# Graph attention on one core: the exponentials go to PSUM alone, and VectorE reads and copies them from there

## The chip, the core and the metric

The kernel runs on one NeuronCore of a Trainium2 chip. The core has TensorE for matrix products, VectorE and ScalarE for elementwise work, GpSimd, here only for issuing gathers, and SyncE, here only for issuing plain transfers. Each engine works through its own queue of instructions in order and waits for others by semaphores. The metric is the device time of one execution in microseconds. Before the change it is 2854.36 us, the median of three runs (2850.2 to 2856.99).

## The reference

A graph of 6250 nodes has 206,250 edges, sorted by the node they end in, with 128 features for each node and each edge, and 8 heads of 16 columns. For each edge a score per head is computed, clipped and exponentiated; the exponentials weigh the source node's values, both are summed by target node and divided, and the result is added to the node's features and normalised.

```python
Qh, Kh, Vh = (h @ WQ), (h @ WK), (h @ WV)          # each reshaped to (N, 8, 16)
Eh = (edge_attr @ WE).reshape(-1, H, D)
score = jnp.einsum('ehd,ehd,ehd->eh', Kh[src], Qh[dst], Eh) * inv_sqrt_d
score = jnp.exp(jnp.clip(score, -5.0, 5.0))
msg = Vh[src] * score[:, :, None]
wV = jax.ops.segment_sum(msg, dst, num_segments=N)
Z = jax.ops.segment_sum(score, dst, num_segments=N)
h_out = wV / (Z[:, :, None] + 1e-06)
...
x = _layernorm(x + h_out.reshape(N, H * D), axis=-1)
```

## The kernel before

A first stage, some 170 us long, projects the nodes and writes tables of K with V and of Q to HBM. The main loop then takes the edges in 403 groups of 512, four tiles of 128 edges each. Its order is written out by hand, engine by engine, and each engine's part is a function `step(g)`.

GpSimd issues four indirect transfers for a group (`gather`, L536), which fetch a row of K and V for each edge into `kv`, a ring of 20 groups. Before the first of them it waits for `msg_ok`, which says that the messages of the group that had that buffer are made. SyncE loads the edge features `attr` (L316) when TensorE has turned older ones, and rows of Q (L322).

In `step(g)` TensorE turns the edge features of group g+2 (L651, to bank `psT`), computes distances to nearby nodes (L659, `psF`), multiplies the turned features of group g+1 by the weights (L667, `psE`), selects rows of Q (L677, `psQ`) and, last, sums the messages of group g-1 by target node (L687, from `hot` and `msg` to the first 136 columns of one of two banks `psW`). That last product waits for `msg_ok`, and it counts `sums` up.

ScalarE copies and marks for group g+2 (L832, L838), takes the exponential of the clipped scores of group g (L844), and prepares `hot`, the 0/1 matrix of targets, for group g+2 (L821 four times, L826).

VectorE multiplies K of group g by the edge product in `psE` (L1056), adds the sums of group g-2 from `psW` to `acc` (L1093 twice), multiplies by the selected Q in `psQ` (L1061), makes the messages of group g-1 (L1077), reduces to scores (L1066) and clips (L1072). Between these stand small instructions of `finish`, which complete one window of 128 nodes in each turn of eight groups. Once in a turn VectorE loads eight window numbers into its registers (L283).

`msg` has two buffers of 4 x 136 columns in SBUF for each partition: 128 columns of messages and 8 of exponentials for each tile. TensorE needs both side by side. Before the change ScalarE writes the exponentials straight into the 8 columns, and VectorE reads them there as the second input of the messages.

Of the kernel before, what the change touches and what calls it, by code (L numbers as in the profile page):

```python
# [5 lines left out]
P = 128  # L6
# [5 lines left out]
ACT = mybir.ActivationFunctionType  # L12
AX = mybir.AxisListType

HEADS = 8
# [11 lines left out]
MSGS = 2  # L27
# [19 lines left out]
def graph_attention_layernorm(nc, x, src, dst, edge_attr, wq, wk, wv, we, out):  # L47
# [12 lines left out]
    n_nodes, dim = x.shape  # L60
    n_edges = src.shape[0]
    TILES = 4
    GROUP = TILES * P
# [6 lines left out]
    DH = dim // HEADS  # L70
    MW = dim + HEADS
    SCALE = float(DH) ** -0.5
# [33 lines left out]
    with ExitStack() as ctx:  # L106
        def sb(name, shape, dt=F32):
            return ctx.enter_context(nc.sbuf_tensor(name, shape, dt))

        def pb(name, shape):  # L110
            return ctx.enter_context(nc.psum_tensor(name, shape, F32))

        def sem(name):
            return ctx.enter_context(nc.semaphore(name))
# [18 lines left out]
        msg = sb("msg", [P, MSGS, TILES, MW])  # L133
        score = sb("score", [P, TILES * HEADS])
        clipped = sb("clipped", [P, TILES * HEADS])
# [51 lines left out]
        psW = pb("psW", [P, 2, GROUP])  # L187
# [65 lines left out]
        exp_ok = sem("exp_ok")  # L253
        msg_ok = sem("msg_ok")
        sums = sem("sums")
# [25 lines left out]
        def load_row(engine, row, g, n, largest):  # L281

            _, values = nc.values_load_multi_w_load_instructions(  # L283
                table[0:1, row, bass.ds(g + COLUMN[row], n)], engines=(engine,), min_val=0, max_val=largest)
            return values

        def per_head(ap):
            return ap.rearrange("p t (h d) -> p t h d", h=HEADS)
# [4 lines left out]
        def _(sp):  # L293
# [36 lines left out]
            def load_bases(g, n):  # L330
                return load_row(mybir.EngineType.SP, BASE, g, n, PARTS * (n_nodes - NEAR))
# [405 lines left out]
        def _(act):  # L737
# [101 lines left out]

            def exponentials(g):  # L840
                act.wait_ge(clip, g + 1)
                if g >= MSGS:
                    act.wait_ge(sums, g - MSGS + 1)
                nc.scalar.activation(msg[:, g % MSGS, :, dim:MW], clipped[:, :].rearrange("p (t h) -> p t h", h=HEADS),  # L844
                                     ACT.Exp, scale=SCALE).then_inc(exp_ok, 1)

            def step(g):
                if g + 2 < G:
                    copy_attr(g + 2)
                    mark_near(g + 2)  # L850
                exponentials(g)
                if g + 2 < G:
                    mark(g + 2)
# [28 lines left out]
        def _(dve):  # L882
# [191 lines left out]

            def messages(g):
                dve.wait_ge(exp_ok, g + 1)
                nc.vector.tensor_tensor(per_head(msg[:, g % MSGS, :, 0:dim]), per_head(kv[:, g % RINGS, :, dim:2 * dim]),  # L1077
                                        msg[:, g % MSGS, :, dim:MW].unsqueeze(3).to_broadcast([P, TILES, HEADS, DH]),
                                        ALU.mult).then_inc(msg_ok, 1)

            def load_windows(g, n):

                half_windows = load_row(mybir.EngineType.DVE, HALF_WINDOW, g, n, 2 * (WIN - 1))
                return [((h + 1) // 2, h // 2) for h in half_windows]
# [58 lines left out]
            def step(g, windows, w=None):  # L1143
                u = g % TURN

                def meanwhile(i):
                    if i == 0 and g >= 2:
                        add_sums(g - 2, windows)
                    if i == 1 and g >= 1:
                        messages(g - 1)  # L1150
                    if w is not None and 3 * u + i < STAGES:
                        finish(3 * u + i, w, 1, window_y[:, :, :], finished, w * STAGES)

                scores(g, meanwhile)
# [17 lines left out]
            for g in range(B_LAST * TURN, G):  # L1172
                step(g, windows[g - B_LAST * TURN])
            messages(G - 1)
            add_sums(G - 2, windows[-2])
            add_sums(G - 1, windows[-1])
# [90 lines left out]
```

## Time and profile before

| What | Value |
|---|---|
| Median of three runs | 2854.36 us |
| The profiled execution's own time | 2860.5 us |
| Its span | 2858.7 us |
| TensorE busy (matrix products) | 1845.5 us, 65% |
| VectorE busy | 1490.2 us, 52% |
| ScalarE busy | 1373.7 us, 48% |
| GpSimd busy | 1581.0 us, 55% |
| Mean granted TensorE clock | 0.743 of full speed |
| Memory traffic | 125 GB/s mean |

A busy time is the sum of an engine's recorded instructions. No engine is busy for more than two thirds of the span, so the time is made of chains between engines, and an average share says little. What is to be read is who waits for whom at each point of a step. A row of a timeline gives the start in us, the duration in us, engine, line, operation, output<-inputs, the count of merged instructions and, in brackets, how long the engine had been idle before and what released it. In a row of a grouped view the two numbers after the bar are total busy us and mean ns of one.

### The profile page before, as it was taken

What the parts mean: (1) busy time and instruction counts of PE and PEld (TensorE: products, weight loads), DVE (VectorE), ACT (ScalarE), POOL (GpSimd) and SP (SyncE); (2) the same over time, 40 slices, a digit from 0 to 9 for tenths busy, and PEclk for the clock granted to TensorE, in tenths of its full rate; (3) what the DMA queues carried; (4) which work ended last, traced back from release to release, by engine and by line L of the source; (5) the groups of instructions that cost most, each with busy time, mean ns of one, the idle gap of its engine ahead of it and who ended that gap; (6) DMA issues with size and microseconds to landing.
All of it is one profiled execution on the core that took longest, in us unless ns stands there. A gap on an engine that the chain in (4) does not pass through costs nothing.

```text
span 2858.7 us, 39244 instructions
## 1 busy us (share of the span) xinstructions
PE 1845.5 (65%) x10440; PEld 1536.1 (54%) x10441; DVE 1490.2 (52%) x3796; ACT 1373.7 (48%) x3309; POOL 1581.0 (55%) x1629
## 2 busy tenths in 40 slices
PE   6266766767667666566666667566656676666676
PEld 5255655555555555455555555455555565555565
DVE  4154455555555555555554555555555555555567
ACT  3144554444544544454444444444444454444455
POOL 7435565555555555555555555555555565555540
PEclk9677677676777777777777777877777777777678
DMA  8335444444444444444444444444444444444431
GB/s 244 104 114 166 126 131 121 124 121 126 126 124 124 125 126 120 122 126 124 121 125 119 120 122 125 127 119 126 124 121 124 118 131 124 122 126 124 122 114 38
DMA packets 281405, 356.25 MB, mean 125 GB/s; under 512 B 144640, under 2 KB 177615, under 8 KB 281186
## 3 DMA queue, kind: packets, MB, share of 16 engines
q0 software_dynamic: 76864, 209.29, 24.9%
q1 hardware_dynamic: 203746, 144.18, 18.1%
q8 instruction: 88, 1.44, 0.2%
q14 instruction: 131, 1.07, 0.1%
q10 hardware_dynamic: 576, 0.26, 0.0%
HBM read 337.59 MB, written 15.97 MB: 124 GB/s over the span
## 4 chain that ended last, share of the span: by engine, by line
PE 61%; issue 33%; another core or an unknown queue 3%; DVE 1%; ACT 1%; DVEq 0%; DMA 0%; SPq 0%; ACTq 0%
PE psW L687 22%; PE psE L667 19%; PE psT L651 9%; PE psF L659 6%; PE psQ L677 4%; PE psE L610 1%; ACT hot L821 0%; PE psW L619 0%; DVE acc L1022 0%; DVE kv L901 0%; DVEq L283 0%; ACT hotT L838 0%; DMA hot<-in_x_dram 0%; ACT q_stage L793 0%
## 5 line engine op out<-in xcount | busy, mean ns | idle before, releaser
L536 POOL DMA_INDIRECT kv<-kv_table,src_idx x1580 | 1539.7, 975 | 1173.2 <-DVE msg L1077 736.8
L687 PE MATMUL psW<-msg,hot 128*128 128x136 f32 x3224 | 677.2, 373 | 891.7 <-issue 889.2
L687 PEld LDWEIGHTS psW<-msg,hot 128*128 128x128 f32 x3224 | 585.9, 264 | 935.4 <-issue 927.8
L1093 DVE TENSOR_TENSOR acc<-psW,acc 64x136 f32 x806 | 239.0, 296 | 860.6 <-remote 668.9
L667 PE MATMUL psE<-w_e,attrT 128*128 128x128 f32 x3224 | 590.6, 339 | 3.0 <-DVE prod L1056 3.0
L832 ACT ACTIVATE attrT<-psT 128x512 f32<-128x512 f32 x403 | 239.8, 595 | 727.8 <-remote 694.1
L667 PEld LDWEIGHTS psE<-w_e,attrT 128*128 128x128 f32 x3224 | 505.5, 239 | 138.8 <-issue 138.8
L821 ACT ACTIVATE hot<-iota,local 128x128 f32<-128x128 f32 x1612 | 509.0, 387 | 0.0
L1056 DVE TENSOR_TENSOR prod<-kv,psE 128x512 f32<-128x512 f32 x403 | 275.7, 684 | 363.1 <-issue 146.1
L844 ACT ACTIVATE msg<-clipped 128x32 f32<-128x32 f32 x403 | 92.3, 229 | 603.7 <-DVE clipped L1072 473.9
L651 PE MATMUL psT<-ident,attr 128*128 128x128 f32 x1612 | 348.1, 357 | 2.1 <-ACT kv L766 0.9
L826 ACT ACTIVATE hot<-hot,one 128x512 f32<-128x512 f32 x403 | 290.9, 722 | 13.1
L651 PEld LDWEIGHTS psT<-ident,attr 128*128 128x128 f32 x1612 | 283.3, 191 | 3.5 <-issue 3.3
L1061 DVE TENSOR_TENSOR prod<-prod,psQ 128x512 f32<-128x512 f32 x403 | 277.2, 688 | 12.6
L838 ACT ACTIVATE hotT<-psF,near_bias 128x512 bf16<-128x512 f32 x403 | 275.4, 683 | 12.3 <-remote 10.5
L1077 DVE TENSOR_TENSOR msg<-kv,msg 128x512 f32<-128x512 f32 x403 | 276.7, 687 | 0.3 <-ACT msg L844 0.3
L1066 DVE TENSOR_REDUCE score<-prod 128x32 f32<-128x512 f32 x403 | 271.4, 673 | 0.0
L659 PE MATMUL psF<-feats,coef 3*128 3x512 bf16 x403 | 201.8, 501 | 2.0 <-ACT hotT L838 1.6
L677 PE MATMUL psQ<-q_near,hotT 128*128 128x128 bf16 x1612 | 175.3, 233 | 18.5 <-issue 17.3
L677 PEld LDWEIGHTS psQ<-q_near,hotT 128*128 128x128 bf16 x1612 | 140.5, 108 | 28.5 <-issue 17.8
L659 PEld LDWEIGHTS psF<-feats,coef 3*128 3x128 bf16 x403 | 38.3, 95 | 107.8 <-issue 104.2
L1072 DVE TENSOR_SCALAR clipped<-score 128x32 f32<-128x32 f32 x403 | 76.7, 190 | 4.6
(111 smaller groups left out, 466.1 us busy)
## 6 DMA issues: line engine op xcount, KB each, us to landing
attr<-in_edge_attr_dram SPq DMA_DIRECT2D x403, 256.0 KB
kv<-kv_table,src_idx POOLq DMA_INDIRECT x1580
q_near<-q_table SPq DMA_DIRECT2D x403, 32.0 KB
kv_table<-kv SPq DMA_DIRECT2D x12, 512.0 KB
q_table<-q_stage SPq DMA_DIRECT2D x12, 384.0 KB
hot<-in_x_dram SPq DMA_DIRECT2D x12, 256.0 KB
xT<-in_x_dram SPq DMA_DIRECT2D x8, 384.0 KB
out_dram<-xT SPq DMA_DIRECT2D x45, 64.0 KB
```

The lines of the kernel that those rows point to most:

```text
L536: nc.gpsimd.indirect_dma_start(out=kv[:, g % RINGS, t, :], out_offset=None, in_=kv_table, in_offset=bass.IndirectOffsetOnAxis(ap=src_idx[: ...
L651: last = nc.tensor.transpose(psT[:, t * P:(t + 1) * P], attr[:, g % ATTRS, t, :], ident[:, :])
L659: nc.tensor.matmul(psF[:, :], coef[:, :], feats[:, g // FEATS % 2, g % FEATS, :], start=True, stop=True)\
L667: last = nc.tensor.matmul(psE[:, g % 2, t * P:(t + 1) * P], attrT[:, g % 2, t * P:(t + 1) * P], w_e[:, :], start=True, stop=True)
L677: last = nc.tensor.matmul(psQ[:, g % 2, t * P:(t + 1) * P], hotT[:, g % 2, t * P:(t + 1) * P], q_near[:, g % QROWS, :], start=True, stop=True)
L687: last = nc.tensor.matmul(psW[:, g % 2, 0:MW], hot[:, g % HOTS, t, :], msg[:, g % MSGS, t, :], start=(t == 0), stop=(t == TILES - 1))
L821: last = nc.scalar.activation(hot[:, g % HOTS, t, :], iota[:, :], ACT.Abs, scale=-1.0, bias=local[:, t, g:g + 1])
L826: nc.scalar.activation(slot, slot, ACT.Relu, scale=-1.0, bias=one[:, 0:1]).then_inc(hot_ok, 1)
L838: nc.scalar.activation(hotT[:, g % 2, :], psF[:, :], ACT.Relu, bias=near_bias[:, 0:1]).then_inc(hotT_ok, 1)
L1056: nc.vector.tensor_tensor(tiles, kv[:, u, :, 0:dim], psE[:, g % 2, :].rearrange("p (t d) -> p t d", d=dim), ALU.mult).then_inc(ke, 1)
L1061: nc.vector.tensor_tensor(prod[:, :], prod[:, :], psQ[:, g % 2, :], ALU.mult).then_inc(keq, 1)
L1077: nc.vector.tensor_tensor(per_head(msg[:, g % MSGS, :, 0:dim]), per_head(kv[:, g % RINGS, :, dim:2 * dim]), msg[:, g % MSGS, :, dim:MW].un ...
```

## The change

ScalarE's exponential no longer writes to `msg` but to PSUM: 32 columns in the second half of the bank `psW[:, g % 2]`, of which TensorE's sums use the first 136 columns. Its wait for `sums`, which protected the `msg` buffer, becomes a wait for `msg_ok`, which protects the new place. In `messages`, VectorE first copies the exponentials from PSUM to the 8 columns of `msg`, and then multiplies, reading the second input from PSUM. Both count nothing more than before: `msg_ok` is counted up by the product.

```diff
+        def exp_scores(g):
+
+            return psW[:, g % 2, GROUP // 2:GROUP // 2 + TILES * HEADS].rearrange("p (t h) -> p t h", h=HEADS)
...
             def exponentials(g):
                 act.wait_ge(clip, g + 1)
-                if g >= MSGS:
-                    act.wait_ge(sums, g - MSGS + 1)
-                nc.scalar.activation(msg[:, g % MSGS, :, dim:MW], clipped[:, :].rearrange("p (t h) -> p t h", h=HEADS),
-                                     ACT.Exp, scale=SCALE).then_inc(exp_ok, 1)
+                scores = clipped[:, :].rearrange("p (t h) -> p t h", h=HEADS)
+                if g >= 2:
+                    act.wait_ge(msg_ok, g - 1)
+                nc.scalar.activation(exp_scores(g), scores, ACT.Exp, scale=SCALE).then_inc(exp_ok, 1)
...
             def messages(g):
                 dve.wait_ge(exp_ok, g + 1)
+                nc.vector.tensor_copy(msg[:, g % MSGS, :, dim:MW], exp_scores(g))
                 nc.vector.tensor_tensor(per_head(msg[:, g % MSGS, :, 0:dim]), per_head(kv[:, g % RINGS, :, dim:2 * dim]),
-                                        msg[:, g % MSGS, :, dim:MW].unsqueeze(3).to_broadcast([P, TILES, HEADS, DH]),
+                                        exp_scores(g).unsqueeze(3).to_broadcast([P, TILES, HEADS, DH]),
                                         ALU.mult).then_inc(msg_ok, 1)
```

On VectorE, this is one step in the main loop before the change, from the product with Q to the next step's first product; `keq`, `exp_ok`, `dot` and `e_mm` are the semaphores waited for:

```order
267 L1061 TENSOR_TENSOR prod<-prod,psQ 128x512 [waits q_sel,ke]
268 L1077 TENSOR_TENSOR msg<-kv,msg 128x4x128 [waits exp_ok]
269 L1066 TENSOR_REDUCE score<-prod 128x32 [waits clip,keq]
270 L1072 TENSOR_SCALAR clipped<-score 128x32 [waits exp_ok,dot]
271 L1056 TENSOR_TENSOR prod<-kv,psE 128x512 [waits kv_in1,e_mm]
```

The same place of VectorE's queue after the change, whose lines are numbered 4 or 5 higher:

```order
286 L1065 TENSOR_TENSOR prod<-prod,psQ 128x512 [waits q_sel,ke]
287 L1081 COPY msg<-psW 128x4x8 [waits exp_ok]
288 L1082 TENSOR_TENSOR msg<-kv,psW 128x4x128
289 L1070 TENSOR_REDUCE score<-prod 128x32 [waits clip,keq]
290 L1076 TENSOR_SCALAR clipped<-score 128x32 [waits exp_ok,dot]
291 L1060 TENSOR_TENSOR prod<-kv,psE 128x512 [waits kv_in1,e_mm]
```

One copy stands new ahead of the messages and has taken over their wait; the messages read `psW` where they read `msg`.

On ScalarE, before the change, the exponential in its step, with what stands ahead of and behind it:

```order
107 L832 ACTIVATE attrT<-psT 128x512 [waits e_mm,attr_tr]
108 L838 ACTIVATE hotT<-psF,near_bias 128x512 [waits q_sel,feat_mm]
109 L844 ACTIVATE msg<-clipped 128x4x8 [waits sums,clip]
110 L821 ACTIVATE hot<-iota,local 128x128 [waits sums]
111 L821 ACTIVATE hot<-iota,local 128x128 x3
112 L826 ACTIVATE hot<-hot,one 128x512 [waits apart]
```

And ScalarE after the change:

```order
107 L836 ACTIVATE attrT<-psT 128x512 [waits e_mm,attr_tr]
108 L842 ACTIVATE hotT<-psF,near_bias 128x512 [waits q_sel,feat_mm]
109 L849 ACTIVATE psW<-clipped 128x32 [waits msg_ok,clip]
110 L825 ACTIVATE hot<-iota,local 128x128 [waits sums]
111 L825 ACTIVATE hot<-iota,local 128x128 x3
112 L830 ACTIVATE hot<-hot,one 128x512 [waits apart]
```

Nothing has moved there; the destination and one of the two semaphores differ. The queues of TensorE, GpSimd and SyncE are unchanged.

## Rows read from the trace of the kernel before

**Rows 1.** Busy windows: stretch, PE, PEld, DVE, ACT, POOL, clock, DMA, GB/s.
```profile
174.00:2751.00 2577.00, 1687.78 (x9525) 1405.93 (x9525) 1347.82 (x3485) 1257.81 (x3050) 1486.32 (x1524) 0.74 0.44 125
2771.00:2841.00 70.00, 54.90 (x417) 45.98 (x418) 60.53 (x156) 50.92 (x129) 0.00 (x0) 0.98 0.19 57
```

**Rows 2.** Waits of GpSimd: who for whom, us, times, longest us.
```profile
POOL kv L536 <- DVE msg L1077: 736.8, 210, 56.5
```

**Rows 3.** Timeline of TensorE, 1626.5 to 1641.5 us.
```profile
1631.41 1.15 PE L687 MATMUL psW<-msg,hot 128*128 128x136 f32 x8
```

**Rows 4.** Timeline of VectorE, 1626.5 to 1641.5 us.
```profile
1628.63 0.61 DVE L1093 TENSOR_TENSOR acc<-psW,acc 64x136 f32 x2 [0.41 <-PE psW L687]
...
1630.20 0.68 DVE L1077 TENSOR_TENSOR msg<-kv,msg 128x512 f32<-128x512 f32 x1
...
1631.71 0.18 DVE L1072 TENSOR_SCALAR clipped<-score 128x32 f32<-128x32 f32 x1
1631.80 0.68 DVE L1056 TENSOR_TENSOR prod<-kv,psE 128x512 f32<-128x512 f32 x1
1638.47 0.61 DVE L1093 TENSOR_TENSOR acc<-psW,acc 64x136 f32 x2 [5.99 <-remote]
```

**Rows 5.** Timeline of GpSimd, 1619 to 1675 us.
```profile
1626.94 0.94 POOL L536 DMA_INDIRECT kv<-kv_table,src_idx  x1 [2.85 <-DVE msg L1077]
...
1635.75 0.95 POOL L536 DMA_INDIRECT kv<-kv_table,src_idx  x1 [0.30 <-issue]
1640.85 0.94 POOL L536 DMA_INDIRECT kv<-kv_table,src_idx  x1 [4.16 <-DVE msg L1077]
...
1654.94 0.94 POOL L536 DMA_INDIRECT kv<-kv_table,src_idx  x1 [3.94 <-DVE msg L1077]
...
1658.68 1.39 POOL L536 DMA_INDIRECT kv<-kv_table,src_idx  x1 [0.30 <-issue]
...
1666.31 0.94 POOL L536 DMA_INDIRECT kv<-kv_table,src_idx  x1 [1.24 <-issue]
...
1674.63 0.94 POOL L536 DMA_INDIRECT kv<-kv_table,src_idx  x1 [3.63 <-DVE msg L1077]
```

**Rows 6.** All gathers, by line and as a group: ns min/median/max.
```profile
L536 POOL DMA_INDIRECT kv<-kv_table,src_idx x1580: 940/946/1450, 57.6 to 2764.4; - x198
...
L536 POOL DMA_INDIRECT kv<-kv_table,src_idx x1580 | 1539.7, 975 | 1173.2 <-DVE msg L1077 736.8 <-issue 431.2 <-DMA kv_table<-kv 5.2
```

**Rows 7.** Timeline of VectorE, 1652 to 1668 us.
```profile
1658.56 0.69 DVE L1077 TENSOR_TENSOR msg<-kv,msg 128x512 f32<-128x512 f32 x1
```

**Rows 8.** Timeline of GpSimd: beginnings of rounds, early and late in the loop.
```profile
221.56 0.94 POOL L536 DMA_INDIRECT kv<-kv_table,src_idx  x1 [2.66 <-DVE msg L1077]
...
232.53 0.94 POOL L536 DMA_INDIRECT kv<-kv_table,src_idx  x1 [1.02 <-DVE msg L1077]
...
430.69 0.94 POOL L536 DMA_INDIRECT kv<-kv_table,src_idx  x1 [4.12 <-DVE msg L1077]
...
444.66 0.94 POOL L536 DMA_INDIRECT kv<-kv_table,src_idx  x1 [4.27 <-DVE msg L1077]
...
2713.72 0.94 POOL L536 DMA_INDIRECT kv<-kv_table,src_idx  x1 [2.84 <-DVE msg L1077]
...
2727.87 0.94 POOL L536 DMA_INDIRECT kv<-kv_table,src_idx  x1 [4.45 <-DVE msg L1077]
...
2740.46 0.94 POOL L536 DMA_INDIRECT kv<-kv_table,src_idx  x1 [2.43 <-DVE msg L1077]
...
2751.84 0.94 POOL L536 DMA_INDIRECT kv<-kv_table,src_idx  x1 [1.24 <-DVE msg L1077]
```

**Rows 9.** Costliest groups: line, shapes, count, busy us, mean ns, idle before.
```profile
L1061 DVE TENSOR_TENSOR prod<-prod,psQ 128x512 f32<-128x512 f32 x403 | 277.2, 688 | 12.6
L1077 DVE TENSOR_TENSOR msg<-kv,msg 128x512 f32<-128x512 f32 x403 | 276.7, 687 | 0.3 <-ACT msg L844 0.3
L844 ACT ACTIVATE msg<-clipped 128x32 f32<-128x32 f32 x403 | 92.3, 229 | 603.7 <-DVE clipped L1072 473.9 <-issue 129.6
```

## The prediction

> **What bounds the kernel now.** I read the busy windows first, then the waits, then one stretch of the timeline engine by engine. In the long middle of the main loop 2577 us pass while 1524 gathers are issued, four to a group: 381 groups at 2577.6 / 381 = 6.77 us. After the last gather the same instructions for 18 groups take 70 us, 3.9 us each [rows 1]. No engine is near full in the middle (TensorE is busy 1688 of 2577 us, at a mean granted clock of 0.74 against 0.98 after it), so most of the 2.9 us of difference is waiting that exists only while gathers are issued. GpSimd in turn waits 210 times for the message product of VectorE, which frees one of the 20 `kv` buffers [rows 2]. So there is a loop between the engines: messages, gathers, and back.
>
> The timeline shows how it closes. TensorE records its sum matmuls from 1631.41 on, for 1.15 us, so they are over at 1632.6; VectorE, which waits for nothing but them, adds them at 1638.47, 5.9 us later [rows 3, 4]. In the step before, the sums were picked up at once (0.41 us of idleness, released by L687) [rows 4]. Something holds back what TensorE has finished. I call such a stretch *held*. It ends 1.6 to 1.8 us after the last gather of a row of eight has been issued (1635.75 + 0.95, against 1638.47 minus some 0.2) [rows 4, 5]. Then comes a fixed chain: add, product with Q, messages, first new gather at 1640.85, 2.4 us after the add [rows 4, 5]. I count time in *rounds*, from one gather that had to wait for messages to the next. Most are pair rounds, of two groups, since the second message is ready before the first four gathers are out: there are 138 from 180 us on, 70 rounds of one group, 11 of three.
>
> **A mechanism that the change touches.** A gather takes 946 ns in the middle, but up to 1450 [rows 6]. All 113 long ones that I found in the main loop begin 0.1 to 0.5 us after a message product has begun: the product at 1658.56, the gather at 1658.68, 1.39 us long [rows 5, 7]. No other large VectorE operation does this. L1077 reads both inputs from SBUF; L1056, L1061 and L1093, which overlap gathers 998 times with never a long one, read one from PSUM. The Trainium skill has it so (SBUF — State Buffer, Who interferes with whom): a VectorE instruction with two SBUF inputs shuts out a GpSimd instruction that reads SBUF. The trace agrees, and by that rule the changed product, with one SBUF input, no longer does it.
>
> What matters is what a long gather does to the hold. Of the 138 pair rounds, 42 have no long gather. 40 of them are held to the end and take 13.9 to 14.2 us: the first of these 430.69 to 444.66, the last 2713.72 to 2727.87, also 1626.94 to 1640.85. (The other two came early, at 256 and 309 us.) It does not matter on which side the product misses the gather's start. 96 have a long gather; 30 of those are held all the same (1640.85 to 1654.94, 14.09), but 66 are let go 0.7 to 3.6 us sooner: the first 221.56 to 232.53, the last 2740.46 to 2751.84, also 1654.94 to 1666.31, 11.37 us [rows 5, 8]. I read this as cause and effect: the 0.44 us gap in the row of gathers lets TensorE's results through.
>
> **The change part by part.**
> - The wait of the exponential (sums of two steps ago) becomes a wait for messages of two steps ago. Both are behind VectorE already when it clips, so nothing is gained or lost. Behind it on ScalarE stand the four L821 and L826; they are as late as before.
> - The exponential, 229 ns [rows 9], writes to PSUM. No row shows that destination; between half and twice 229 ns it stays hidden, since its result is read a whole step later and VectorE waited for it 0.3 us in all [rows 9]. I take 0.
> - The message product reads its second input from PSUM. L1061 does so in 688 ns, L1077 without it in 687 [rows 9]: 0 us. The repeated read of one PSUM column has no row of its own; these two lie 1 ns apart, and I allow 0.03 us to either side, an estimate (about 5% of them), within the range of the next item.
> - One more VectorE instruction in each of 403 groups, a copy of 32 columns, right ahead of the product for which GpSimd and TensorE wait. The nearest row is L1072, also 32 columns, 0.18 us long, with the next instruction beginning 0.09 us after it [rows 4]. Nothing waits between copy and product, so I take 0.10 us; bounds 0.06 and 0.20 us. There is no cover for it at the end of a round: the chain add, Q product, messages is alone there. It is paid once a round, and the second product in a pair round has slack.
> - The long gathers go. Directly that is 1580 x (975 - 946 ns) = 46 us of GpSimd [rows 6, 9], but a held pair round takes 13.97 us without and 14.09 us with one, so the gain is nearer 0.1 than 0.44 us a round. What goes with them is the early release.
>
> **The sum.** All rounds become held pair rounds of 13.97 + 0.10 = 14.07 us, 7.04 us a group. The rounds of one group mostly go too: 1666.31 to 1674.63 (8.32 us) follows an early release [rows 5], and when four pairs make up eight groups, VectorE's load of window numbers falls into the hold. 381 x (7.04 - 6.77) = +103 us, and 18 x 0.1 = +2 us at the end. The profiled execution took 2860.5 us, span 2858.7; it would take 2965. The timed runs have their median 6 us lower: **2959 us**, +3.7%. If the rounds of one group stay, eight groups take three pairs and two singles, 3 x 14.07 + 7.6 + 8.4 = 58.2 us or 7.28 a group, +195 us; but early releases may survive now and then as in 2 of 42, so I leave the value where it is.
>
> At this place the skill speaks against my reading of the hold. The same section states that TensorE and ScalarE never wait on anyone and that DMA never contends with a compute engine. The trace does not agree: 5.9 us between the end of a sum and its pick-up, only while gathers run. By the page the sum would have the copy and the shorter gathers alone, which is near the first two rivals.
>
> **Rivals.**
> 1. *Only the copy counts.* The early releases come from where the steps stand in time, not from the long gather, and stay as frequent. Then 219 rounds x 0.10 = +22 us, with 0.20 a copy +44 us: 2876 us (2867 to 2898). For it: 30 rounds with a long gather are held. Against it: 40 of 42 against 30 of 96.
> 2. *The gathers are the bound, and the change is faster.* A hold ends a fixed time after the last gather, so 0.44 us less of gathers ends it 0.44 us sooner. Price: 107 rounds x 0.43 = -46 us, +22 for the copy: -24 us, 2830 us. It decides if a release follows the last gather's end also where the gather was long; the rows with 13.97 and 14.09 us speak against it, the three-group rounds, in which it would be 0.8 us, for it.
> 3. *Another rhythm, much better.* The 0.1 us shifts the steps so that more pair rounds are let go early, at 11.4 to 12.6 us. At 12.0 for all: 6.0 a group, -290 us, near 2565 us. Nothing in the rows without a long gather points there.
> 4. *Worse:* single rounds stay, about 3055 us.
>
> **Chances.** Forecast 0.60; rival 1 0.18; rival 2 0.11; rival 3 0.04; rival 4 0.07. The runs shown differ by 0.24%, so I take 0.2% as the least difference that can be told from none. Rival 1 is slower by 0.8%, with some 0.04 below 0.2%; so slower 0.80, same 0.05, faster 0.15. The likeliest case alone spans 2920 to 2995 (copy 0.06 to 0.20, a few early releases kept). The range is 2850 to 3000: it takes in rival 1 and leaves out 2, 3 and 4.
>
> **What would show it.** Right, if no gather is longer than about 1 us; if nearly all waits of GpSimd for messages come 14 us apart, some 190 of them and not 210; if the copy begins 0.10 us ahead of the product; and if the stretch after the last gather grows by no more than 2 us. Wrong in its main step, if pair rounds of 11.4 or 12.6 us remain without long gathers (rival 1), or held ones fall to 13.6 us (rival 2).

## The result, and the profile after

The changed kernel took 2949.4 us (median of four runs, 2943.7 to 2959.5) against 2853.4 us for the kernel before: a ratio of 1.034, 95% interval 1.031 to 1.037. It is slower by 3.4%; the forecast was 2959 us, 3.7%. The profiled execution took 2943.7 us, the fastest of the four; its span is 2942.0. On which chip this pair ran is not on record; its 2853.4 us is close to the 2857.7 us of the first chip below.

First the busy windows of the changed kernel, with the same columns as in [rows 1]:

```profile
174.00:2830.00 2656.00, 1618.01 (x9525) 1358.73 (x9525) 1378.68 (x3860) 1263.09 (x3049) 1445.22 (x1524) 0.74 0.43 121
2850.00:2925.00 75.00, 59.30 (x422) 50.14 (x423) 62.90 (x177) 51.26 (x130) 0.00 (x0) 0.91 0.18 53
```

The same 1524 gathers now fill 2656 us, so a group takes 2656 / 381 = 6.97 us in place of 6.77 [rows 1]: +79 us in the long middle. GpSimd's own busy time fell in it, from 1486 to 1445 us. Next the gathers as a group, then the exponential, the copy and the message product, in the view that has total busy us and mean ns behind the bar:

```profile
L540 POOL DMA_INDIRECT kv<-kv_table,src_idx x1580 | 1499.0, 949 | 1290.5 <-DVE msg L1082 855.2 <-issue 431.3 <-DMA kv_table<-kv 4.0
L1082 DVE TENSOR_TENSOR msg<-kv,psW 128x512 f32<-128x512 f32 x403 | 272.6, 677 | 0.0
L849 ACT ACTIVATE psW<-clipped 128x32 f32<-128x32 f32 x403 | 81.0, 201 | 637.2 <-DVE clipped L1076 422.0 <-issue 111.5 <-DVE msg L1082 103.8
L1081 DVE COPY msg<-psW 128x32 f32<-128x32 f32 x403 | 73.8, 183 | 0.3 <-ACT psW L849 0.3
```

None of the instructions that the change touches became longer, and the copy is new: the mean gather went from 975 to 949 ns [rows 6], the message product from 687 to 677, the exponential from 229 to 201 [rows 9]. What grew is the waiting. Of the changed kernel's waits (who for whom, us, times, longest):

```profile
POOL kv L540 <- DVE msg L1082: 855.2, 192, 57.3
DVE acc L1098 <- remote: 854.2, 190, 6.0
ACT attrT L836 <- remote: 767.1, 191, 4.5
```

GpSimd waits for messages 192 times where it was 210 [rows 2], and for 118 us more. The second row is the hold itself: VectorE is ready to add a sum that TensorE has recorded as done, and nothing in the trace but a late signal stands between. The third row shows the same for ScalarE, which waits nearly as long for the edge features that TensorE has turned; before, that row was 694.1 us in 186 waits. So the hold is not something between TensorE and VectorE alone. One such round, first TensorE's sum, then VectorE, then the rounds' beginnings on GpSimd:

```profile
1576.68 1.15 PE L691 MATMUL psW<-msg,hot 128*128 128x136 f32 x8
```

```profile
1576.66 0.69 DVE L1060 TENSOR_TENSOR prod<-kv,psE 128x512 f32<-128x512 f32 x1
1583.07 0.61 DVE L1098 TENSOR_TENSOR acc<-psW,acc 64x136 f32 x2 [5.72 <-remote]
...
1584.50 0.18 DVE L1081 COPY msg<-psW 128x32 f32<-128x32 f32 x1
1584.60 0.68 DVE L1082 TENSOR_TENSOR msg<-kv,psW 128x512 f32<-128x512 f32 x1
```

```profile
1571.44 0.95 POOL L540 DMA_INDIRECT kv<-kv_table,src_idx  x1 [4.33 <-DVE msg L1082]
...
1580.21 0.95 POOL L540 DMA_INDIRECT kv<-kv_table,src_idx  x1 [0.30 <-issue]
1585.55 0.95 POOL L540 DMA_INDIRECT kv<-kv_table,src_idx  x1 [4.39 <-DVE msg L1082]
...
1599.75 0.94 POOL L540 DMA_INDIRECT kv<-kv_table,src_idx  x1 [4.34 <-DVE msg L1082]
```

The sum is over at 1577.83 and is picked up 5.2 us later. The rounds here last 14.11 and 14.20 us, as the held ones of before did (1640.85 to 1654.94, [rows 5]).

Now the counts over the main loop. After 174 us no gather is above 1.02 us, where 115 were (113 in the prediction, which drew no sharp line); the three longer ones that the changed kernel has lie at 62 to 77 us, in the first stage. For the rounds I begin a new one when GpSimd has been idle for 0.6 us or more ahead of a gather, and call a round held if VectorE picks up its last sums at least 11.2 us after its first gather. By this rule, which shifts some of the prediction's counts by one:

| | before | changed |
|---|---|---|
| pair rounds, held (mean us) | 70 (14.01) | 165 (14.09) |
| pair rounds, early (mean us) | 67 (11.98) | 24 (13.01) |
| rounds of one group (mean us) | 70 (7.93) | 1 (7.4) |
| rounds of three groups (mean us) | 12 (19.77) | 0 |

The table tells where the +79 us come from. It is an estimate from the counts and means above. The 67 early rounds at the new held length cost 67 x 2.11 = +141 us, the 70 held ones 70 x 0.08 = +6, the 12 rounds of three groups 12 x 1.37 = +16. The 70 rounds of one group were the costliest for a group, 7.93 us against 7.04 in a held pair, and their going gives 70 x 0.89 = 62 us back. The 24 early rounds that are left give 24 x 1.08 = 26. Together that is +75. So the change took away short pair rounds, which costs, and rounds of one group, which gains, and the first weighed more.

### The profile page after: what moved, and what is told of

Read it like the earlier page. It is cut to its first block, busy times and chain, and to the rows that moved or that the text cites. A ratio compares the mean times of both kernels' runs of the same rounds, so it can differ in the third digit from the quotient of the medians.

```text
span 2942.0 us, 39647 instructions
## 1 busy us (share of the span) xinstructions
PE 1778.6 (60%) x10440; PEld 1492.0 (51%) x10441; DVE 1524.3 (52%) x4199; ACT 1379.2 (47%) x3309; POOL 1541.3 (52%) x1629
## 4 chain that ended last, share of the span: by engine, by line
PE 59%; issue 37%; another core or an unknown queue 2%; DVE 1%; ACT 1%; DMA 0%; DVEq 0%; SPq 0%; ACTq 0%
PE psW L691 22%; PE psE L671 18%; PE psT L655 9%; PE psF L663 6%; PE psQ L681 3%; PE psE L614 1%; PE psW L623 0%; DVE acc L1026 0%; DVE kv L905 0%; DMA hot<-in_x_dram 0%; ACT q_stage L797 0%; ACT q_stage L791 0%; DVEq L283 0%; PE psF L600 0%
## 5 line engine op out<-in xcount | busy, mean ns | idle before, releaser
L540 POOL DMA_INDIRECT kv<-kv_table,src_idx x1580 | 1499.0, 949 | 1290.5 <-DVE msg L1082 855.2
L671 PE MATMUL psE<-w_e,attrT 128*128 128x128 f32 x3224 | 554.4, 324 | 3.2 <-DVE prod L1060 3.2
L671 PEld LDWEIGHTS psE<-w_e,attrT 128*128 128x128 f32 x3224 | 472.4, 225 | 132.1 <-issue 132.1
L849 ACT ACTIVATE psW<-clipped 128x32 f32<-128x32 f32 x403 | 81.0, 201 | 637.2 <-DVE clipped L1076 422.0
L655 PE MATMUL psT<-ident,attr 128*128 128x128 f32 x1612 | 338.4, 350 | 1.4 <-ACT kv L770 0.9
L655 PEld LDWEIGHTS psT<-ident,attr 128*128 128x128 f32 x1612 | 276.9, 187 | 2.1 <-issue 2.1
L1082 DVE TENSOR_TENSOR msg<-kv,psW 128x512 f32<-128x512 f32 x403 | 272.6, 677 | 0.0
L663 PE MATMUL psF<-feats,coef 3*128 3x512 bf16 x403 | 194.8, 483 | 0.0
L681 PE MATMUL psQ<-q_near,hotT 128*128 128x128 bf16 x1612 | 164.8, 227 | 0.8 <-DMA q_near<-q_table 0.8
L681 PEld LDWEIGHTS psQ<-q_near,hotT 128*128 128x128 bf16 x1612 | 134.0, 104 | 8.8 <-DMA q_near<-q_table 1.3
```

Source lines behind the costliest of these rows:

```text
L540: nc.gpsimd.indirect_dma_start(out=kv[:, g % RINGS, t, :], out_offset=None, in_=kv_table, in_offset=bass.IndirectOffsetOnAxis(ap=src_idx[: ...
L655: last = nc.tensor.transpose(psT[:, t * P:(t + 1) * P], attr[:, g % ATTRS, t, :], ident[:, :])
L663: nc.tensor.matmul(psF[:, :], coef[:, :], feats[:, g // FEATS % 2, g % FEATS, :], start=True, stop=True)\
L671: last = nc.tensor.matmul(psE[:, g % 2, t * P:(t + 1) * P], attrT[:, g % 2, t * P:(t + 1) * P], w_e[:, :], start=True, stop=True)
L681: last = nc.tensor.matmul(psQ[:, g % 2, t * P:(t + 1) * P], hotT[:, g % 2, t * P:(t + 1) * P], q_near[:, g % QROWS, :], start=True, stop=True)
```

## Experiments

They ran on three chips, four kernels on each, always beside the kernel before on the same chip. The changed kernel itself, without clears, was not run on the second and third. The medians of the kernel before were 2857.7 us on the first, 2933.4 on the second and 2096.3 on the third. Ratios go by these. The difference between the chips turned out to be part of the answer.

**1. Exponentials in both places, no copy (first chip).** The message product reads PSUM; TensorE reads what ScalarE wrote to SBUF; VectorE copies nothing. ScalarE waits for both `sums` and `msg_ok` ahead of its two writes (not shown in the cut).

```diff
-                nc.scalar.activation(msg[...dim:MW], clipped[...], ACT.Exp, scale=SCALE).then_inc(exp_ok, 1)
+                nc.scalar.activation(msg[...dim:MW], scores, ACT.Exp, scale=SCALE)
+                nc.scalar.activation(exp_scores(g), scores, ACT.Exp, scale=SCALE).then_inc(exp_ok, 1)
...
-                                        msg[:, g % MSGS, :, dim:MW].unsqueeze(3).to_broadcast(...)
+                                        exp_scores(g).unsqueeze(3).to_broadcast(...)
```

> Before, with one thing changed: ScalarE writes each group's exponentials twice, to the messages in SBUF (for TensorE's sums) and to PSUM, and VectorE's message product takes them from PSUM. There is no copy on VectorE. My theory (the product's second input in SBUF makes one gather long, and the gap that this leaves lets TensorE's finished results through early): the long gathers are gone, nearly every pair round has its results held and lasts about 13.97 us (the held rounds before), without the copy's 0.10 us; the time is about 2930 us (2905 to 2950). Rival 1 (only the copy's time on VectorE's chain costs): there is no copy, so the time is that of before, 2845 to 2862 us. Rival 2 (what counts is at which moment VectorE's steps fall, which ScalarE's second write of about 0.2 us moves by a little): some shift of a few tens of us either way, with the pair rounds still of both kinds.

Measured: 2953.0 us (2949.6 to 2959.3), ratio 1.034 (1.031 to 1.037). The gathers and VectorE's wait for sums:

```profile
L540 POOL DMA_INDIRECT kv<-kv_table,src_idx x1580 | 1498.6, 948 | 1299.1 <-DVE msg L1083 866.1 <-issue 426.9 <-DMA kv_table<-kv 6.1
DVE acc L1099 <- remote: 892.7, 191, 6.2
```

No copy, and the whole loss. No gather of the main loop is above 1.02 us; 185 of 189 pair rounds are held, at 14.01 us, which is the length of the held rounds before. So the loss comes with the product's second input in PSUM, not with the copy. The median is 3 us above my range, which had left room for early rounds: there were four. "Only the copy costs" falls.

**2. The copy alone (first chip).** The kernel before, with a copy of 32 columns from PSUM to a scratch tile ahead of the product.

```diff
+                if 1 <= g < G - 1:
+                    nc.vector.tensor_copy(spent[:, :], psW[:, (g + 1) % 2, 0:TILES * HEADS])
```

> Before, with one thing added: VectorE copies 32 columns of PSUM to a scratch tile in SBUF ahead of each message product, which itself reads both inputs from SBUF as before. Its output is the reference's. My theory: the long gathers (113) and the early releases stay, and only the held rounds are longer by 0.10 to 0.2 us: 2855 to 2885 us. Rival (the 0.1 to 0.2 us by which the product comes later is what moves the rounds out of the early release, not the operands' place): near the changed kernel, 2925 to 2960 us, with few early rounds although long gathers remain.

Measured: 2871.8 us (2863.8 to 2895.2), ratio 1.0056 (1.0032 to 1.0081). The gathers' group and the waits:

```profile
L537 POOL DMA_INDIRECT kv<-kv_table,src_idx x1580 | 1513.0, 958 | 1217.5 <-DVE msg L1080 774.9 <-issue 437.9 <-DMA kv_table<-kv 4.7
DVE acc L1096 <- remote: 757.2, 159, 6.4
```

14 us, a seventh of the change's loss. The size is right, and one point fell: I had written that the long gathers stay, and 58 of 115 are left. That the copy moves the product against the gathers, so that it meets fewer of them, is a guess. In the pair rounds the link to the long gathers is tighter than before: 52 with a long one last 12.32 us in the mean, 126 without one 14.05. Of these 126, which have both inputs in SBUF, 117 are 13.7 us or longer like those of the changed kernel, so the hold needs no product that reads PSUM. With half of the long gathers gone one might expect half of the loss. Here too the costly rounds go: those of one group fall from 70 to 16, while the early pair rounds fall only from 67 to 56.

**3. One gap a group (first chip).** The changed kernel; GpSimd clears 384 columns of a scratch tile (0.435 us) before the gather of each group's last tile.

```diff
+            def rest():
+                nonlocal pauses
+                if pauses:
+                    pool.wait_ge(paused, pauses)
+                pauses += 1
+                nc.gpsimd.memset(pause[:, :], 0.0).then_inc(paused, 1)
...
+                    if t in (3,):
+                        rest()
                     nc.gpsimd.indirect_dma_start(
```

> The changed kernel, with one thing added: GpSimd clears a scratch tile of 384 columns (by its instructions of the kind some 0.4 us) ahead of the first gather of the last tile of each group, and waits for that clear before the next pause. It leaves GpSimd idle of gathers for some 0.4 us once a group. My theory (a gap in the stream of gathers lets the held results through): more of the pair rounds release early, at about 8.6 to 11 us after their start where now it is 11.3 to 11.5, and the kernel is faster than the changed one, by 50 to 250 us, although GpSimd has more to do. Rival (gaps do nothing, the length of a gather had another meaning): the same as the changed kernel or up to 0.45 us a group slower, 2949 to 3130 us.

Measured: 2814.9 us (2804.6 to 2825.0), ratio 0.985 (0.980 to 0.989), so some 135 us faster than the changed kernel's 2949.4, with 172 us more work for GpSimd. Timeline of GpSimd, then of VectorE, around one release:

```profile
1519.10 0.94 POOL L553 DMA_INDIRECT kv<-kv_table,src_idx  x1 [3.80 <-DVE msg L1095]
...
1522.54 0.44 POOL L525 MEMSET pause<- 128x384 f32 x1
...
1526.89 0.95 POOL L553 DMA_INDIRECT kv<-kv_table,src_idx  x1 [0.30 <-issue]
1527.84 0.43 POOL L525 MEMSET pause<- 128x384 f32 x1
1528.43 0.95 POOL L553 DMA_INDIRECT kv<-kv_table,src_idx  x1 [0.16 <-issue]
1531.96 0.94 POOL L553 DMA_INDIRECT kv<-kv_table,src_idx  x1 [2.57 <-DVE msg L1095]
```

```profile
1529.29 0.61 DVE L1111 TENSOR_TENSOR acc<-psW,acc 64x136 f32 x2 [4.30 <-remote]
```

The sum is picked up 1.45 us after the second clear begins, while the last gather is still being issued. In the changed kernel it comes 1.9 us after the last gather is over (1580.21 + 0.95 against 1583.07). The round (1519.10 to 1531.96) is 12.86 us long, with a longer row of gathers. Not all rounds gain: 75 of 178 pair rounds are still held (14.08 us long), and 103 are let go early (12.48 us). In these the sums are picked up 8.7 to 10.9 us after the round's start, about as I had expected (8.6 to 11).

**4. Four gaps a group (first chip).** The same clear before every gather: `if t in (0, 1, 2, 3)`.

> The changed kernel with the same clear of 384 columns ahead of each tile's gathers (four a group in place of one). My theory: four gaps a group release the results wherever they are ready, so that the rounds are no longer held until the gathers end; GpSimd's own work is then 8 x 0.6 us of gathers and 4 x 0.43 us, some 6.6 us a group, and the time is 2700 to 2900 us. Rival (gaps do nothing): GpSimd's 1.7 us a group come on top of the 6.99 us of a group: 3300 to 3600 us.

Measured: 2535.4 us (2529.8 to 2548.5), ratio 0.889 (0.885 to 0.892). It is faster than my theory had it. Groups and timeline of GpSimd:

```profile
L553 POOL DMA_INDIRECT kv<-kv_table,src_idx x1580 | 1510.6, 956 | 255.6 <-issue 193.3 <-POOL pause L525 61.3 <-DVE msg L1095 1.0
L525 POOL MEMSET pause<- 128x384 f32 x1580 | 687.7, 435 | 1.7 <-issue 0.8
```

```profile
1509.14 0.96 POOL L553 DMA_INDIRECT kv<-kv_table,src_idx  x1 [0.16 <-issue]
1510.10 0.43 POOL L525 MEMSET pause<- 128x384 f32 x1
1510.70 0.95 POOL L553 DMA_INDIRECT kv<-kv_table,src_idx  x1 [0.16 <-issue]
```

GpSimd waits for messages 1.0 us in all, where it was 855, and the late pick-ups of VectorE and ScalarE (<- remote) have no row in the waits any more. Only GpSimd's own work is left: a gather each 1.55 us, four a group, 381 groups: 2362 us. This is what shows that the hold hangs on the gathers' close succession. 688 us of useless work made the kernel some 414 us faster than the changed one. Between gap and rate this run does not tell apart: a longer gap also means fewer gathers in a given time.

**5. A clear too short to widen the gap (second chip).** 16 columns (128 ns) before every gather.

> The changed kernel with a clear of 16 columns (an estimate of 0.12 us, from 205 ns for 128 columns and 515 for 512) ahead of each of a group's four pairs of gather instructions' tiles, so that each gather still begins about 1.25 us after the one before, as in the changed kernel: there is another instruction in the gap, but the gap is not longer. If the gap's length decides what is held: no release early, 2935 to 2965 us. If any instruction of another kind between two gathers does it: the rounds are no longer held, and with 5.0 us of gathers a group the time falls far below that of the pause of 384 columns, 2150 to 2450 us.

Measured: 3017.9 us, ratio 1.029 (1.027 to 1.032). This chip is slower as a whole (2933 us before), so the ratio is to be read: 2935 to 2965 us was 1.028 to 1.039 on the first chip. The waits of GpSimd, now at the clear ahead of the gather, and of VectorE:

```profile
POOL pause L525 <- DVE msg L1095: 849.7, 191, 40.0
DVE acc L1111 <- remote: 740.4, 191, 6.1
```

The ratio rests on the guess that the plain change costs the same here. The rounds need no such guess: gathers are 1.26 us apart and all 190 pair rounds are held, at 14.32 us. An instruction of another kind that leaves the gathers' spacing as it was does nothing.

**6. A middle clear (second chip).** 192 columns (273 ns), gathers 1.39 us apart.

> The changed kernel with a clear of 192 columns (an estimate of 0.27 us) ahead of every gather, so that gathers follow each other at some 1.38 us in place of 1.25 (and of 1.55 with 384 columns). If this gap is long enough: GpSimd is the bound at 5.5 us a group, 381 groups in 2103 us, and with the 145 us outside the main loop and 22 of its tail 2270 us, or 2250 to 2420 if other engines come in. If it is too short: rounds held as in the changed kernel, each longer by the pauses, 2950 to 3080 us. Between the two if it lets only some of the held results through.

Measured: 2801.1 us (2798.5 to 2832.3), ratio 0.958 (0.952 to 0.964). The waits:

```profile
POOL pause L525 <- DVE msg L1095: 382.1, 121, 18.9
DVE acc L1111 <- remote: 477.6, 175, 5.3
```

In between, as the third branch had it: the pick-ups are late nearly as often as before (175 times) but by 2.7 us in the mean, where the changed kernel has 4.5.

**7. The kernel before with four gaps (second chip).** As in 4, on the kernel before.

> The kernel before (exponentials in SBUF, no copy) with the clear of 384 columns ahead of every gather. With the results no longer held, the change's own cost should be gone too if my theory is right, because GpSimd's 6.2 us a group is the bound in both: within 1% of the changed kernel with the same pauses (2535 us), 2515 to 2570. If the second input in SBUF costs something by itself, the gathers show it: up to 0.44 us more for each gather that a product meets, one a group, 381 x 0.44 = 168 us at most: up to 2700.

Measured: 2547.9 us (2539.7 to 2559.8), ratio 0.868 (0.864 to 0.871). GpSimd waits for messages 0.8 us in all. The two kernels with these clears are within 0.5% of each other in us, though on two chips; without them they are 3.4% apart. This speaks for the cost being in the hold; the pair on one chip comes with 9 to 12.

**8. Two gaps a group (second chip).** `if t in (1, 3)`, 384 columns.

> The changed kernel with the clear of 384 columns ahead of the gathers of the second and the fourth tile alone (two a group). GpSimd's work is 2 x 1.25 + 2 x 1.55 = 5.6 us a group. If a gap every 2.8 us is enough: 381 x 5.6 = 2134 us, with the 167 outside 2300 us, up to 2450 when a result has to wait up to 2.8 us for the next gap. If the gaps are needed as often as in the kernel with four: between it and the kernel with one gap a group (2535 and 2815 us).

Measured: 2785.0 us (2771.4 to 2810.9), ratio 0.950 (0.943 to 0.956). My first branch (2300 to 2450) fell; the second, between four gaps and one, came true. The waits are 462 us of GpSimd and 381 us of VectorE: a gap every 2.8 us does not let everything through; one at every gather does. Experiments 6 and 8 together bear on gap or rate. In a row without waits the gathers follow each other at 1.39 us in 6 and at (2 x 1.25 + 2 x 1.55) / 4 = 1.40 us in 8, with gaps of 0.43 us everywhere against 0.60 us at every second gather. Their times differ by 0.6%, and the single runs overlap (2798 to 2832, 2771 to 2811). So the mean spacing describes both as well as the gap does, and a reading in which only the rate of gathers counts is not excluded.

**9 to 12. Finer lengths, and one partition (third chip).** Clears before every gather: 288 columns on the changed kernel and on the kernel before, 384 columns on one partition (`pause[0:1, :]`), 240 columns.

> The changed kernel with a clear of 288 columns ahead of every gather (an estimate of 0.36 us from 273 ns for 192 columns and 435 for 384), so that gathers follow each other at 1.47 us. If the results come through whenever GpSimd leaves 0.51 us between two gathers: GpSimd is the bound with 5.9 us a group, 381 x 5.9 = 2248 us and 167 outside: 2415 us, up to 2470. If the length wanted lies between 0.51 and 0.60 us: results held in part, as with 192 columns, 2550 to 2820 us.

> The kernel before with the same clear of 288 columns ahead of every gather. If the change costs only through what is held, this equals the changed kernel with 288 columns within 1% (2415 to 2470 us where the gap is long enough). If the gap of 0.51 us is a little too short, the long gathers (the product's second input in SBUF) should help this kernel and it should be the faster of the two by 1 to 5%.

> The changed kernel with the clear of 384 columns ahead of every gather on 1 partition in place of 128: the same length in time, 1/128 of the data written. If the gap's length in time is what counts, the same as with 128 partitions, about 0.889 of the kernel before (2520 to 2560 us). If the amount that GpSimd writes in the gap counts, the results stay held: 2950 us or more.

> The changed kernel with a clear of 240 columns (an estimate of 0.32 us, gathers 1.43 us apart) ahead of every gather, between 192 columns (0.958 of the kernel before) and 288. If more gap steadily lets more through, 0.86 to 0.95 of the kernel before; if there is a length from which all results come through and 0.48 us is below it, near the 0.958 of 192 columns; if it is above it, GpSimd's 5.7 us a group bind: 381 x 5.7 = 2172 and 167 outside, 2340 us, 0.82.

| Third chip | us | ratio (95%) | gathers apart, us |
|---|---|---|---|
| changed, 288 | 2396.9 | 1.1425 (1.141 to 1.144) | 1.47 |
| before, 288 | 2413.9 | 1.151 (1.150 to 1.153) | 1.47, some 1.9 |
| changed, 384, one partition | 2480.1 | 1.182 (1.181 to 1.184) | 1.52 |
| changed, 240 | 2333.2 | 1.113 (1.111 to 1.114) | 1.43 |

In us all four came within 1.6% of the lowest value expected without a hold (2415, 2415, 2520 and 2340); the ratios are the opposite of what I had expected, since here the kernel before, without any gap, takes 2096.3 us. None of the four traces of this chip has a late pick-up in its waits. Nor is there room for one in the time of the kernel before. In the kernel with 240 columns, 1524 gathers take 2175 us, and some 158 us lie outside them; take 158 from 2096.3, and the kernel before issues a gather each 1.272 us. By itself a gather could follow each 1.25 us (as in the timelines of the changed kernel), and its long ones raise the mean by 975 - 949 = 26 ns: 1.276. So a gather bound accounts for the kernel before here; it is an estimate, since its trace on this chip was not taken. Gaps then only cost. The experiments on length and on one partition therefore tell nothing of the hold: which length suffices on the first two chips, between 0.43 us (in part) and 0.60 (all), stays open.

The pair on the third chip shows the change without the hold:

```profile
L553 POOL DMA_INDIRECT kv<-kv_table,src_idx x1580 | 1507.0, 954 | 254.9 <-issue 192.8 <-POOL pause L525 58.3 <-DVE msg L1095 3.9
```

```profile
L549 POOL DMA_INDIRECT kv<-kv_table,src_idx x1580 | 1524.0, 965 | 254.9 <-issue 192.8 <-POOL pause L521 57.3 <-DVE msg L1090 4.8
```

The first row is of the changed kernel, the second of the kernel before, both with 288 columns. The gathers differ by 17.0 us in total, the times by 17.0 us: where GpSimd's issuing is the bound, the change makes the kernel 0.7% faster, by as much as its gathers are shorter. I expected them within 1%, and they are; the other branch, in which the kernel before is the faster by 1 to 5%, fell. So without a hold the change costs nothing. The two plain kernels were not compared on this chip, so whether the change is faster there is not shown.

## Why the prediction was right, point by point

- **Long gathers go.** Right: none is left in the main loop, where there were 115. Before, 118 gathers began while a message product ran, and 115 of them were long; in the changed kernel 145 did, and none. The Trainium skill (SBUF — State Buffer, Who interferes with whom) gives the rule for two SBUF inputs; experiment 1 agrees: 154 gathers began during a product with one SBUF input, and none was long. One count of mine was wrong: gathers do overlap the other three large operations while they are long. The one at 1658.68 runs into L1056, and 47 such overlaps are in the trace. What holds is that of 341 gathers that began during those three one was long.
- **The early releases go with them.** The main step, and right: 67 early rounds became 24, and 4 in experiment 1. That long gathers and early releases belong together was a reading of 40 in 42 against 30 in 96; experiment 1 shows it by taking the long gathers away, and experiments 3 to 6 show that more room between gathers shortens the hold. The Trainium skill's statements in the same section (SBUF — State Buffer, Who interferes with whom), that TensorE and ScalarE never wait on anyone and that DMA never contends with a compute engine, do not account for what the first two chips did: late pick-ups of 854 us in the changed kernel, none when gathers are 1.55 us apart. On the third chip no run contradicts them.
- **How a long gather does it.** Here the prediction's picture, that the gap of 0.44 us lets finished results through, does not fit its own trace. The prediction's early round from 1654.94 on:

```profile
1659.38 1.15 PE L687 MATMUL psW<-msg,hot 128*128 128x136 f32 x8
...
1663.74 0.61 DVE L1093 TENSOR_TENSOR acc<-psW,acc 64x136 f32 x2 [3.01 <-remote]
```

  The long gather ends at 1660.07 [rows 5], the sum only at 1660.53, and it is picked up at 1663.74, three gathers further on. So the sum was not there to pass while the gap was. Of the kernel before's 162 late pick-ups 59 came while gathers were still being issued. In all 59 the sum ended after the last long gather, and most were picked up 3.6 to 3.8 or 5.0 to 5.3 us after that gather's end. With clears it is another picture: in experiment 6 all 113 such sums were over before the last clear ended, and 103 of them were picked up 0.7 to 0.9 us after it. A long gather must act by something that lasts longer than the gap. Time lost to the row of gathers, which is the reading by rate, would fit; no run here shows it, and the cause of the hold stays open.
- **The copy.** 0.10 us from start to start (1584.50 to 1584.60), as taken. Held rounds are 14.09 us long with it and 14.01 without (experiment 1). But its net cost in this kernel can't be told from nothing: 1.034 with it and 1.034 without, since the kernel with the copy keeps 24 early rounds against 4. Why these survive without a long gather is not settled.
- **The sum.** +103 us expected in the middle, +79 measured. The 24 early rounds account for the difference, 24 x 1.08 = 26 us; I had put them at nothing. That the median came as near as 10 us has some luck in it: between the profiled executions the difference is only 83 us, and between the medians 96, where 105 were forecast.
- **The end.** +2 us expected. From the last gather to the end of the span it was 2858.7 - 2764.4 = 94.3 us [rows 6], and is 2942.0 - 2841.5 = 100.5: +6. The granted clock is 0.91 of full speed in that stretch against 0.98 [rows 1]. The term was mis-sized, by 4 us.
- **Counts.** 192 waits where about 190 were named, 14 us apart; single rounds gone but for one of 70.
- **The smaller items.** The exponential and the product were taken at no change and became 28 and 10 ns shorter. No run separates what that is worth.
- **Rival 1** (copy alone) is what experiment 2 measures: +0.56%, below its +0.8%. **Rival 2** (gathers are the bound, faster) is wrong for the chip on which the prediction was tested and right in kind for the third, where the gathers bind once clears are in both kernels. **Rival 3** (many more early rounds) and **rival 4** (single rounds stay) did not come about. To rival 2 I gave 0.11 as a case of the same chip; that another chip could decide between the two I had not seen, and no profile of one chip shows it.

## What to carry to other kernels

An instruction that is slowed by a contention can still go with a faster kernel: before removing the contention, count which rounds have it and how long these last. When an engine waits for a signal whose sender is recorded as done, and only while gathers are issued back to back, try a pause between the gathers before anything else; here 0.43 us of useless clearing before each gather gave 11 and 13% against the kernel before on the first two chips. Then try it on more than one chip: on the third, clears of 0.32 to 0.41 us cost 11 to 18%, so none of these versions is simply the better kernel.

## What the runs showed of the hardware that was not expected

- The same kernel took 2096, 2858 and 2933 us on three chips, each number stable within 0.4% on the third and 0.6% on the others. By the estimate above, in which the gathers alone account for the 2096 us, the 761 us between the first and the third come with the hold. What differs between the chips no run here shows.
- On the first two chips VectorE picks up TensorE's finished sums late when gathers follow each other at 1.25 to 1.26 us (190 and 191 late pick-ups), in part at 1.39 (175, shorter), and not at 1.55 (no row). ScalarE's pick-ups behave alike (191, 191 and 205, no row).
- A GpSimd gather that begins while VectorE runs a product with both inputs in SBUF takes up to 1450 ns in place of 946 (115 of 118); with one of them in PSUM, none of 145 did.
- Clears on GpSimd: 128 ns for 16 columns, 273 for 192, 315 for 240, 355 for 288, 435 for 384; on one partition 384 columns still take 408.
- ScalarE's exponential of 128x32 takes 201 ns to PSUM and 229 to SBUF. In experiment 1, which writes both, one right behind the other, it takes 229 ns to SBUF and then 183 to PSUM.
